# A state-space block on one core: first products moved beside their scans, sums first on TensorE, normalisation moved from VectorE to ScalarE

## The reference, cut to what matters

```python
xn = layer_norm(group_norm(x), norm_g, norm_b)        # per position, over 512 channels
# for each of 4 chunks of 128 channels:
xi, z = in_proj(xn)                                   # 256 channels each
xc = silu(causal_conv4(xi) + conv_b)
dt_low, Bs, Cs = x_proj(xc)                           # 8, 16 and 16 rows
dt = softplus(dt_proj(dt_low) + dt_proj_b)
h[s] = exp(dt * A[s]) * h[s] + (dt * xc) * Bs[s]      # 16 states s, along the positions
y = (sum over s of h[s] * Cs[s] + xc * D) * silu(z)
chunk_out = out_proj(y) + skip_scale * xn_chunk
out = x + proj(layer_norm(all chunks)) + proj_b
```

## Time and profile before

| | us |
|---|---|
| median of 3 runs | 19080.81 |
| lowest and highest | 19080.58, 19089.64 |
| the profiled execution, its own time | 19076.83 |
| its span, first to last instruction | 19075.0 |
| busy: GpSimd, VectorE, TensorE, ScalarE | 15748.1, 15622.9, 15127.4, 10618.6 |

### The profile page before, as it was taken

The page is one execution under the profiler, slowest core; times in us unless marked ns, Lnnn a source line. Parts: engine busy times, 40 slices in busy tenths (PEclk is TensorE's granted clock), DMA queues, the critical chain, the costliest instruction groups (busy, mean ns, idle before and its releaser), DMA issues. The chain is left out here.

```text
span 19075.0 us, 159023 instructions
## 1 busy us (share of the span) xinstructions
PE 15127.4 (79%) x30720; PEld 6007.8 (31%) x30720; DVE 15622.9 (82%) x13443; ACT 10618.6 (56%) x17724; POOL 15748.1 (83%) x6524
## 2 busy tenths in 40 slices
PE   6888878888788887888878878788787887878887
PEld 2333323333233332333323333233332333333333
DVE  7888868888688886888868888688886888868887
ACT  4555545555455554555545555455554555545655
POOL 5888868888688886888868888688886888868988
PEclk8888888888888888888888888888888888989998
DMA  3444434444344443444434444334443344434433
GB/s 127 137 138 140 142 108 137 139 140 141 108 138 138 140 141 108 138 139 139 141 109 137 140 138 142 109 136 140 139 141 109 136 139 140 140 109 138 138 137 125
DMA packets 739067, 2535.98 MB, mean 133 GB/s; under 512 B 77240, under 2 KB 78016, under 8 KB 721728
## 3 DMA queue, kind: packets, MB, share of 16 engines
q1 hardware_dynamic: 738112, 2527.45, 38.8%
HBM read 2376.15 MB, written 150.99 MB: 132 GB/s over the span
## 5 line engine op out<-in xcount | busy, mean ns | idle before, releaser
L1169 POOL TENSOR_TENSOR RING<-RING,CS 128x1024 f32<-128x1024 f32 x4096 | 10001.3, 2451 | 2083.9 <-DVE RING L869 1459.3
L869 DVE TENSOR_TENSOR_SCAN RING<-DA,HS,RING 128x512 f32<-128x512 f32 x8192 | 9984.9, 1265 | 1613.8 <-ACT DA L627 1152.4
L365 PE MATMUL YP<-RING,EYE 128*128 128x512 f32 x16384 | 8531.3, 653 | 1635.3 <-POOL RING L1169 1634.5
L627 ACT ACTIVATE DA<-ITEM,AN 128x512 f32<-128x512 f32 x8192 | 5561.6, 687 | 6111.6 <-DVE RING L869 6102.0
L365 PEld LDWEIGHTS YP<-RING,EYE 128*128 128x128 f32 x16384 | 3253.3, 207 | 6643.0 <-issue 3850.7
L1156 POOL TENSOR_TENSOR RING<-ITEM,BS 128x1024 f32<-128x1024 f32 x1536 | 3644.7, 2373 | 1.1
L849 DVE TENSOR_TENSOR RING<-DTP,BS 128x1024 f32<-128x1024 f32 x2560 | 3124.7, 1221 | 469.9 <-issue 277.4
L365 PE MATMUL FL<-XN,WC 128*128 128x512 f32 x4096 | 2045.9, 647 | 629.0 <-DVE XN L913 618.1
L1174 POOL TENSOR_TENSOR ITEM<-ITEM,EX 128x1024 f32<-128x1024 f32 x256 | 600.8, 2347 | 1046.9 <-ACT EX L674 1046.9
L365 PEld LDWEIGHTS FL<-XN,WC 128*128 128x128 f32 x4096 | 849.8, 210 | 1785.0 <-issue 1712.9
L365 PE MATMUL FL<-LS,WP 128*128 128x512 f32 x2048 | 1075.9, 661 | 319.6 <-DVE YB L881 270.7
(11 more groups left out here) (119 smaller groups left out, 10700.6 us busy)
## 6 DMA issues: line engine op xcount, KB each, us to landing
BS<-bc_rows SPq DMA_DIRECT2D x2048, 512.0 KB, 4.8
CS<-bc_rows SPq DMA_DIRECT2D x2048, 512.0 KB, 3.5
XR<-in_x SPq DMA_DIRECT2D x128, 1024.0 KB, 7.2
x_slices<-XR SPq DMA_DIRECT2D x64, 1024.0 KB, 8.0
XR<-x_slices SPq DMA_DIRECT2D x64, 1024.0 KB, 7.4
out<-XR SPq DMA_DIRECT2D x64, 1024.0 KB, 7.7
ITEM<-in_wqkv SPq DMA_DIRECT2D x24, 1024.0 KB, 5.6
bc_rows<-ROWS SPq DMA_DIRECT2D x256, 64.0 KB, 4.5
```

The source lines that it names most:

```text
L365: return pe.matmul(*a, **k)
L627: act.activation(DA[:, h, :], DT[:, i % 2, h, :], ACT.Exp, scale=AN[:, h, s:s + 1]).then_inc(dA_ready, 1)
L869: dve.tensor_tensor_scan(H[:, slot(n), h, :], DA[:, h, :], U[:, slot(n), h, :], HS[:, i % ITEMS, h, s:s + 1], ALU.mult, ALU.add).then_inc( ...
L1169: pool.tensor_tensor(G[:, slot(n)], H[:, slot(n)], CS[:, s % C_ROWS, :].unsqueeze(1).broadcast_to([P, NH, T]), ALU.mult).then_inc(g_ready, 1)
```

## The change

- **TensorE.** `state_sum(n - 2)` is now the first thing of step s, ahead of the front's work. The product D*xc, which opened YP and came before the first sum, is added in step 9 (`d_term`). `z_both` goes from step 3 to 2, so it stands ahead of the first sum of the item.
- **VectorE.** `make_u(n)` stands right ahead of `scan(n)`; only U of step 5 is made one step early. `gate` goes from after scan pair 2 to after scan pair 3. `apply_norm` and the halo's copy are gone, and so is the wait for `skip_ready`.
- **ScalarE.** The front's pieces stand one step earlier, `silus` (which waits for the gate) among them. It takes over the halo (`keep_halo`) and the normalisation's affine part (`apply_norm`), in step 15 of j = 2 and steps 0 and 4 of j = 3.
- **GpSimd.** `POOL_U` is (2, 4, 6, 8, 10, 12); `dt_first`, `dt_sum`, `dt_x` go from steps 10, 11, 12 to 11, 12, 13. The square is kept in YZ instead of DTX.
- **SyncE.** The rows of the next item are stored after q = 3 instead of q = 4.

```diff
-POOL_U = (0, 1, 3, 5, 7, 9)
+POOL_U = (2, 4, 6, 8, 10, 12)
+EARLY_U = (5, 4)
...
-            return 9 if j in (1, 2) else 7
+            return (6, 8, 9, 6)[j]
...
-                    if front and q == 4:
+                    if front and q == 3:
                         store_rows(tile, w + 1)
...
-                if s == 0:
-                    if not first:
-                        pe.wait_ge(yz_ready, tile * ITEMS + i)
-                    for h in range(NH):
-                        mm(YP[:, h, :], DD[:, h, :], XC[:, i % 2, h, :], start=True, stop=False)
+                if s == 0 and not first:
+                    pe.wait_ge(yz_ready, tile * ITEMS + i)
                 pe.wait_ge(g_ready, tile * STEPS + n + 1)
                 for h in range(NH):
-                    last = mm(YP[:, h, :], EYE[:, :], G[:, slot(n), h, :], start=False, stop=(s == NS - 1))
+                    last = mm(YP[:, h, :], EYE[:, :], G[:, slot(n), h, :], start=(s == 0), stop=(s == NS - 1))
                 last.then_inc(g_summed, 1)
...
+                    if front and s == 2:
+                        z_both(tile, w + 1)
+                    if s > 1 or not first:
+                        state_sum(tile, n - 2, first=first and s == 2)
+                    if s == 9:
+                        d_term(w)
...
-                if not first:
-                    act.wait_ge(u_pool, tile * (NP_U * ITEMS) + NP_U * i)
-                act.activation(DTX[:, :, :], EM[:, :, :], ACT.Square, bias=CUBE_SHIFT, scale=CUBE).then_inc(square_ready, 1)
+                if not first:
+                    act.wait_ge(out_ready, tile * ITEMS + (i - 1))
+                act.activation(YZ[:, :, :], EM[:, :, :], ACT.Square, bias=CUBE_SHIFT, scale=CUBE).then_inc(square_ready, 1)
...
+            def keep_halo():
+                act.activation(XN[:, :, 0:HALO], XN[:, :, T:T + HALO], ACT.Copy).then_inc(halo_kept, 1)
+            def apply_norm(v, ks):
+                act.wait_ge(scaled1, v)
+                act.wait_ge(halo_kept, v)
+                for k in ks:
+                    act.activation(XN[:, k, HALO:HALO + T], LV[:, k, :], ACT.Identity, bias=NBI[:, k:k + 1],
+                                   scale=NG[:, k:k + 1]).then_inc(xn_ready, 1)
...
-                        if s == 4:
+                        if s == 3:
                             if not first:
                                 act.wait_ge(yz_ready, tile * ITEMS + w)
                             silus(tile, w + 1)
...
-                        if s == 8:
-                            dt_split(tile, w + 1, 1)
+                        if s == 7:
+                            dt_split(tile, w + 1, 1)
                             dt_exp(tile, w + 1)
...
-                for m in (n + 1, n + 2):
-                    if m == n + (1 if m % STEPS == STEPS - 1 else 2) and (front or m // NS == n // NS):
-                        make_u(tile, m, first=first)
+                if n % NS != EARLY_U[0]:
+                    make_u(tile, n, first=first)
+                if n % NS == EARLY_U[1]:
+                    make_u(tile, n + EARLY_U[0] - EARLY_U[1], first=first)
...
-                    if s == 2 and not first:
+                    if s == 3 and not first:
                         gate(tile, w - 1)
...
-                        if s == 15:
-                            apply_norm(ahead + 2)
...
-                        if s == 10:
-                            dt_first(tile, w + 1)
                         if s == 11:
-                            dt_sum(tile, w + 1)
+                            dt_first(tile, w + 1)
                         if s == 12:
+                            dt_sum(tile, w + 1)
+                        if s == 13:
                             dt_x(tile, w + 1)
```

More of the change, by code:

```diff
@@ L369, in state_sum, with d_term @@
                 i, s = n // NS, n % NS
-                if s == 0:
-                    if not first:
-                        pe.wait_ge(yz_ready, tile * ITEMS + i)
-                    for h in range(NH):
-                        mm(YP[:, h, :], DD[:, h, :], XC[:, i % 2, h, :], start=True, stop=False)
+                if s == 0 and not first:
+                    pe.wait_ge(yz_ready, tile * ITEMS + i)
                 pe.wait_ge(g_ready, tile * STEPS + n + 1)
                 for h in range(NH):
-                    last = mm(YP[:, h, :], EYE[:, :], G[:, slot(n), h, :], start=False, stop=(s == NS - 1))
+                    last = mm(YP[:, h, :], EYE[:, :], G[:, slot(n), h, :], start=(s == 0), stop=(s == NS - 1))
                 last.then_inc(g_summed, 1)
+            def d_term(i):
+                for h in range(NH):
+                    mm(YP[:, h, :], DD[:, h, :], XC[:, i % 2, h, :], start=False, stop=False)
             def xi_half(tile, i, h):
@@ L441, in window @@
                             front_left(tile, w)
-                            if j == 3:
-                                pe.wait_ge(xn_ready, ahead + 2)
+                            pe.wait_ge(xn_ready, tile * ITEMS + w + 2)
                             xi_half(tile, w + 1, 0)
@@ L494, in window @@
                             proj(3, (2, 3))
+                        if s == 15:
+                            pe.wait_ge(final_ready, (ahead - 1) * NCH + NCH)
                     if j == 2 and ln1:
@@ L510, in window @@
                         out_proj(tile, w - 1)
-                    if s > 1 or not first:
-                        state_sum(tile, n - 2, first=first and s == 2)
-                    if j == 1 and ln2 and s == NS - 1:
-                        pe.wait_ge(final_ready, (ahead - 1) * NCH + NCH)
             def attention(b):
@@ L759, in window @@
                             rstd(var1_ready, log1_ready, rstd1_ready, ahead + 2)
+                        if s == 15:
+                            keep_halo()
+                            apply_norm(ahead + 2, (0,))
+                    if j == 3 and ln1:
+                        if s == 0:
+                            apply_norm(ahead + 2, (1,))
+                        if s == 4:
+                            apply_norm(ahead + 2, (2, 3))
             def attention(b):
@@ L794, in first_front @@
                 rstd(var1_ready, log1_ready, rstd1_ready, tile + 1)
+                apply_norm(tile + 1, range(NCH))
                 xi_copy(tile, 0, 0)
@@ L889, in dt_poly @@
                 dve.wait_ge(square_ready, tile * ITEMS + i + 1)
-                dve.scalar_tensor_tensor(out=DTX[:, :, :], in0=DTX[:, :, :], scalar=13.0 / 16, in1=EM[:, :, :],
+                dve.scalar_tensor_tensor(out=YZ[:, :, :], in0=YZ[:, :, :], scalar=13.0 / 16, in1=EM[:, :, :],
                                          op0=ALU.add, op1=ALU.mult).then_inc(poly_ready, 1)
@@ L906, in scale_norm @@
                                   ALU.mult).then_inc(scaled1, 1)
-            def apply_norm(v):
-                dve.wait_ge(scaled1, v)
-                dve.wait_ge(halo_kept, v)
-                for k in range(NCH):
-                    last = dve.tensor_scalar(XN[:, k, HALO:HALO + T], LV[:, k, :], NG[:, k:k + 1], NBI[:, k:k + 1],
-                                             ALU.mult, ALU.add)
-                last.then_inc(xn_ready, 1)
             def finish(o, v, tail=False):
@@ L949, in window @@
                     n = w * NS + s
-                    make_ahead(tile, n, first=first, front=front)
+                    make_ahead(tile, n, first=first)
                     scan(tile, n, first=first)
-                    if s == 2 and not first:
+                    if s == 3 and not first:
                         gate(tile, w - 1)
@@ L960, in window @@
                             dt_poly(tile, w + 1)
-                    if j == 0 and ln2 and s == 12:
+                    if j == 0 and ln2 and s == 11:
                         centre(YB, mu2_ready, cen2_ready, ahead)
                     if j == 1 and ln2:
-                        for at, o in ((8, 0), (12, 1), (14, 2), (15, 3)):
+                        for at, o in ((8, 0), (12, 1), (13, 2), (15, 3)):
                             if s == at:
@@ L1075, in first_front @@
                 centre(LV, mu1_ready, cen1_ready, tile + 1)
-                scale_norm(tile + 1, first=True)
-                apply_norm(tile + 1)
+                scale_norm(tile + 1)
                 dt_small(tile, 0)
```

72 lines of the change are left out of this document (32 added, 40 removed).

## The result

The changed kernel took 19767.1 us, median of 4 runs (19748.3 to 19774.4), against 19080.7 us beside it: ratio 1.0357, 95% interval 1.0341 to 1.0373. The profiled execution is the shortest of the four, with a span of 19746.5 us, 671.5 more than before.

The account below looks back on a forecast made before the run. No engine is full; waits that keep GpSimd still bound the kernel. 56 x (3.0 + 2.5) = 308 plus 8 x 9.6 = 77 gives +385 on 19076.8: 19460 us, range 18750 to 19860.

Parts of the forecast that it names:

- the second rival: TensorE at half clock in every item: 3 x 2.1 us more a tile, 34 outside, 19850 us; chance 0.20.
- The first rival: Waits covered by GpSimd's queue, idle at most 7.1 us an ordinary period; only tile's end gains: 18630 us, chance 0.23.
- the walk: An ordinary item's price in the new order, timed from D, the end of `dt_x`: period 67.3 us.
- hole at `silus`: VectorE, after the gate: decay of step 4 stands behind `silus`, leaving a hole of 2.9 us.
- I count it at j = 2 alone: TensorE's low clock for the first two sums after the gate, charged only at j = 2: +2.5 us.
- +0.7 for `finish`: Addition at j = 1 for `finish`, beside 1.7 for the projection before the second `dt_split`: period 69.7 us.
- The loop's jump: Start of j = 2: 5.87 us pass on VectorE before its first product, +6.7; period 78.2 before the clock's 2.5.
- Outside the loop: Four items an image: clean item (no extra work) +4.6, two others +4 and +1, last nothing; 8 x 9.6 = 77 us.
- -8.0 us at j = 3: Tile's end: halo copy and affine parts leave VectorE's path for ScalarE, the sure gain of 8.0 us a tile.
- The D product lies in TensorE's slack: D product moved to step 9 on TensorE, counted at nothing.
- Sums first relabels steps: TensorE's sum at each step's head: from sum 1 on fronts follow the same sums as before; counted at nothing.
- nine operations left: GpSimd, from scan 9's end to the next `dt_x`: nine operations instead of seven, 21.8 us.

Follow-up runs that it names:

- kernel 11: The changed kernel with the z projection computed three times over in its place ahead of the gate: 19607.6 us, ratio 1.0275 to the kernel before.
- kernel 2: The kernel before with halo copy and affine part moved to ScalarE and the D product moved to step 9: 18335.0 us, ratio 0.9606.
- kernel 6: The changed kernel with gate, z and ScalarE's whole front back at their old steps: 19069 us, ratio 0.9991 to the kernel before.
- 3: kernel 2 plus the change's placing of products, dt_first, dt_sum and dt_x one step later, square in YZ: 18986.1 us, ratio 0.9947.
- kernel 10: The changed kernel with the placing of products undone, dt_first, dt_sum and dt_x back at steps 10 to 12: 19849.1 us, ratio 1.0402.
- kernel 7: The changed kernel with only VectorE's gate back after scan pair 2: 19047 us, ratio 0.9980 to the kernel before.

## Why the prediction was right, and where it was wrong

The sign and the range held: I gave 19460 in 18750 to 19860. But the time lies beside the second rival (19850), not the forecast: the loss is 686 us and I had 385. The range held because it was wide and took in the slow clock; several of its terms were off and partly cancelled, which is luck. The first rival's condition fails: GpSimd stands still for 10.9 us of an ordinary period, not 7.1 or less.

**Along the walk.** Forecast and measured: scan 15 at D + 1.8 and 1.8; hand-over 0.28 and 0.28; gate's end D + 19.5 and 19.1; hole at `silus` 2.9 and 2.90; from `dt_split` to scan 3.0 and 3.0. Scan 8 came at D + 41.6 instead of 39.2, because the second `dt_split` came 19.5 us after the gate instead of 16.7. Those 2.8 us are the twelve records in 8.14 us instead of 5.41 (the 16.7 had them at full clock).

**"I count it at j = 2 alone"** is the step that failed. I read the earlier trace rows as a wait of 3.19 us at full clock behind it and took ordinary gates to be on that side, and I walked every kind from a gate of j = 1, which had waited 1.31 us. But the row of 4.41 us and half clock is a gate of j = 0, so that kind had paid for the low clock all along. In the trace after, the pause of 3.53 us at j = 0 gives 8.14, pauses of 2.28 give 7.11 at j = 3 and at half of the j = 2 gates, and one of 2.54 gives 5.41. With z ahead of the gate the pauses of j = 1 and 3 grew from 1.31 to 2.28 us, and those of j = 0 and 2 became shorter. The Trainium skill ("TensorE: Matmul & The Clock Gate", section "Part 1: The HAM clock gate") has the rule that an idle array drops to half clock; the trace agrees with it at ordinary gates too, 8.14 against 5.31 us with the pause filled.

The rival's "every item" is not what happened either, so the nearness of 19850 is in part chance. Against full clock the second `dt_split` comes later by 2.8 us at j = 0, 1.8 at j = 3, 1.8 in about half of the turns of j = 2, and 0.6 at j = 1 (19.0 us after the gate instead of 18.4): some 6 us a tile, where I had 2.5 and the rival 8.8.

**"+0.7 for `finish`" at j = 1** left out another wait. The walk gave 69.7, measured were 72.5, and 72.9 with the clock held up (kernel 11), so most of it is not the clock. From the start of scan 8 to the period's end the walk had 28.8 us (69.7 less 40.9), the trace 31.1. In it stands this, on GpSimd and on VectorE:

```profile
3326.07 2.35 POOL L1178 TENSOR_TENSOR RING<-RING,CS 128x1024 f32<-128x1024 f32 x1 [2.15 <-DVE RING L894]
...
3326.60 2.37 DVE L910 TENSOR_SCALAR EM<-EM 128x1024 f32<-128x1024 f32 x1
```

`dt_small` (L910) takes 2.37 us here and 0.67 at j = 0, 2 and 3, and ScalarE's square waits for it. The clean item has it too: the walk gave 65.6, kernel 11 measured 67.7 and the change 70.7.

**The loop's jump** was priced too high. I carried over 5.87 us in front of VectorE's first product; the row of waits above has 111.3 us in 48 times, 2.3 each. So j = 2 came out at 75.0 to 78.2, not 80.7. This takes back part of what the clock and `dt_small` add: per tile 5.5 us forecast, 8.8 over the 56 turns (mostly 7.0 and 10.2, by turns). The periods before also repeat less than I said: in the last image j = 2 and 3 are some 3.5 us shorter. **Outside the loop** I was low: 9.6 us an image against 23 (the clean item +9.7, its neighbours +5.8, +6.1 and +1.3).

**"-8.0 us at j = 3"**: right in kind; alone it gave 571 us instead of 448, 488 of them at j = 3 and most of the rest at j = 0.

**"The D product lies in TensorE's slack"**: true where it went, not where it came from. Taking it from behind the gate was worth 175 us (kernel 2), which I counted at nothing. **"Sums first relabels steps"** is right for most of the front. What is left of TensorE's order, with the earlier store and a few norm pieces, is kernel 6 against 3: 83 us.

**The products** cost 651 us where the rest is on time, by another chain than mine. I held "nine operations left" instead of seven on GpSimd for the cause; putting `dt_x` back, which adds an operation behind it, returned 93 of 651 us. The chain over product 15 and the copy of dtx, which my walk did not have, the hand-overs and the stretched `dt_small` remain.

**The parts together**, each measured on top of those before it: norm -571, D product -175, placing of products +651, the rest of TensorE's order +83, the gate and ScalarE's shift +698: +686, from 19081 to 19767. Taken in another order they have other sizes (kernel 10). So the change holds two gains of 746 us and three losses of 1432.

Open: why pauses of 2.3 to 2.5 us end at full clock in one item and not in the next; how much of kernel 7's 720 us is the clock, which it also keeps up at j = 0 (5.31 to 5.37 us for the twelve records); and what a `dt_small` placed elsewhere would give back. None was tried.

## What to carry to other kernels

In a ring of engines that wait for each other, find the engine whose waits add up with a constant to the time of every version; here span = 17,000 us + GpSimd's waits, within 55. Undo the parts one by one from the good side as well as from the bad: an edit that looks free beside a larger fault cost 651 us once that fault was gone. A reader placed directly ahead of its consumer also delays whoever may overwrite what it reads; and work moved ahead of a wait can lengthen the pause there, behind which TensorE's clock may be at its low level.

## What the runs showed of the hardware that I had not expected

- The copy of 12 values a partition took 2082 ns on VectorE and 196 ns on ScalarE. The Trainium skill ("SBUF — State Buffer", section "Who interferes with whom") says that VectorE's copies can need a port pair that GpSimd holds for a whole instruction; the traces fit that: each of the 56 copies began while a GpSimd instruction of 2.35 us ran and ended 0.03 us after it, and ScalarE's copy shows nothing of it. It holds for `dt_small`, one `tensor_scalar` on VectorE, as well: in the changed kernel a GpSimd instruction was running at its start in the 64 cases of 2.36 to 2.49 us, `dt_small` ended 0.55 us behind that instruction in each, and none was running in the 192 cases of 0.67. No run took GpSimd away from beside them.
- A scan that waits for a product of its own engine mostly starts 0.28 us after it, 1632 times in the run with 0.6 at most, though the order on the engine is fixed: 490.6 us of the run.
- More work can be less time: 4 more projection matmuls in each item's pause, 160 us less.
